# DLRM tower on one core: the feature products of four samples on quarters of the TensorE array instead of halves, in batches twice as large, and the first unit's gather ids loaded by themselves

## What is computed

```
e = jnp.stack([tbl_0[ids[:, 0]], ..., tbl_25[ids[:, 25]]], axis=1)
combined = jnp.concatenate([e, r_dense_x[:, None, :]], axis=1)
interact = jnp.einsum('bfd,bgd->bfg', combined, combined)
z = interact[:, _TRIU_I, _TRIU_J]
h = jnp.concatenate([z, r_dense_x], axis=1)
h = jnp.maximum(h @ W_top1 + b_top1, 0.0)
h = jnp.maximum(h @ W_top2 + b_top2, 0.0)
y = h @ W_top3
```

## Time and profile before

| | us |
|---|---|
| time, median of 3 runs | 375.73 (374.99 to 376.73) |
| time of the profiled execution | 375.79 |
| its span in the trace | 373.8 |
| PE busy | 333.4 (89%) |
| PEld busy | 315.3 (84%) |
| DVE busy | 247.8 (66%) |
| ACT busy | 203.4 (54%) |
| POOL busy | 252.8 (68%) |

### The profile page before, as it was taken

How to read it: one execution, slowest core, us unless ns; L and a number is a source line. 1 busy time by engine, 2 the same in 40 slices (tenths; PEclk the granted TensorE clock), 3 DMA queues, 4 the chain that set the end, 5 groups by cost and what they waited for, 6 DMA issues and landing times.

```text
span 373.8 us, 9779 instructions
## 1 busy us (share of the span) xinstructions
PE 333.4 (89%) x4178; PEld 315.3 (84%) x4178; DVE 247.8 (66%) x298; ACT 203.4 (54%) x274; POOL 252.8 (68%) x262
## 2 busy tenths in 40 slices
PE   0768759969999899989999999989998999989967
PEld 0768649869899898989899998989898989988955
DVE  3999805994469835895389735995389645980324
ACT  1575475425756448536755456645855466548322
POOL 3888777877777777777777777777777777760000
PEclk9998979989999999999999999999999999999989
DMA  7995324453154532563254623563255524420310
GB/s 238 392 322 166 97 59 132 107 156 84 51 131 121 162 81 69 155 184 85 53 155 100 175 63 91 143 180 80 56 155 147 136 51 119 113 72 2 87 39 0
DMA packets 32377, 44.92 MB, mean 120 GB/s; under 512 B 18791, under 2 KB 20463, under 8 KB 32334
## 3 DMA queue, kind: packets, MB, share of 16 engines
q1 hardware_dynamic: 23080, 25.82, 24.0%
q0 software_dynamic: 8192, 16.79, 17.6%
q10 hardware_dynamic: 1062, 1.69, 1.4%
HBM read 38.07 MB, written 6.20 MB: 118 GB/s over the span
## 4 chain that ended last, share of the span: by engine, by line
PE 49%; DVE 21%; POOL 10%; issue 8%; DMA 6%; SPq 3%; ACT 2%; ACTq 0%; DVEq 0%
DVE hot L689 18%; PE ps_gram L458 14%; POOL emb L402 10%; PE ps_mix L476 10%; PE ps_feat L440 7%; PE ps_feat L441 7%; PE ps_feat L426 4%; PE ps_mix L510 3%; DMA products_dram<-gram 3%; SPq L329 3%; ACT feat L588 1%; DMA idx<-in_ids 1%; PE ps_mix L515 1%; PE ps_feat L476 1%; PE ps_mix L525 1%
## 5 line engine op out<-in xcount | busy, mean ns | idle before, releaser
L402 POOL DMA_INDIRECT emb<-in_tbl,idx x256 | 252.1, 985 | 81.7 <-issue 76.8
L689 DVE TENSOR_TENSOR hot<-ids_row,ps_rows 128x1024 fp32r<-128x1024 int32 x160 | 186.2, 1215 | 19.1 <-PE ps_feat L441 16.1
L440 PE MATMUL ps_feat<-hot,held_h 128*128 128x256 f32 x640 | 164.8, 295 | 15.5 <-DVE held_l L675 11.7
L588 ACT COPY feat<-ps_feat 128x512 f32<-128x512 f32 x104 | 125.7, 1229 | 76.6 <-PE ps_feat L426 44.5
L441 PE MATMUL ps_feat<-hot,held_l 128*128 128x256 f32 x640 | 159.6, 287 | 0.0
L440 PEld LDWEIGHTS ps_feat<-hot,held_h 128*128 128x128 f32 x640 | 125.0, 195 | 17.8 <-issue 14.8
L441 PEld LDWEIGHTS ps_feat<-hot,held_l 128*128 128x128 f32 x640 | 125.2, 196 | 0.0
L458 PEld LDWEIGHTS ps_gram<-feat 128*54 128x54 f32 x2048 | 56.0, 132 | 9.7 <-issue 5.4
L458 PE MATMUL ps_gram<-feat 128*54 128x54 f32 x2048 | 61.0, 217 | 1.3 <-ACT feat L588 1.3
L426 PE MATMUL ps_feat<-ident,emb 128*128 128x128 f32 x256 | 40.8, 283 | 9.0 <-DMA emb<-in_tbl,idx 9.0
L603 ACT COPY gram<-ps_gram 119x432 f32<-119x432 f32 x64 | 35.2, 550 | 9.6 <-PE ps_gram L458 9.5
(11 more groups left out here) (101 smaller groups left out, 248.4 us busy)
## 6 DMA issues: line engine op xcount, KB each, us to landing
ids_row<-in_ids_h SPq DMA_DIRECT2D x40, 256.0 KB, 3.9
products_dram<-gram SPq DMA_DIRECT2D x30, 189.0 KB
held_raw<-in_held SPq DMA_DIRECT2D x8, 512.0 KB, 13.1
emb<-in_tbl,idx POOLq DMA_INDIRECT x256
z_raw<-products_dram SPq DMA_DIRECT2D x84, 26.0 KB
held_raw<-in_held ACTq DMA_DIRECT2D x2, 512.0 KB, 9.2
dense<-in_dense_t SPq DMA_DIRECT2D x8, 128.0 KB
w1z_raw<-in_W_top SPq DMA_DIRECT2D x3, 234.0 KB
```

The costliest lines, as they stand in the source:

```text
L402: pool.indirect_dma_start(emb[:, h, f, :], None, table, bass.IndirectOffsetOnAxis(ap=idx[:, i * UNIT + h, f:f + 1].bitcast(u32), axis=0),) ...
L440: nc.tensor.matmul(dst, held_h[:, o, c, :], hot[:, n % 2, c, :], start=c == 0, stop=False)
L588: nc.scalar.copy(feat_v[:, f, b], src).then_inc(act_out, 1)
L689: nc.vector.tensor_tensor(hot[:, n % 2, chunks, :], bass.AP(ids_row, (n % SLOTS) * UC, [[SLOTS * UC, HR], [0, PC], [1, UC]]), row_nums[:, ...
```

## The change

Three edits. The array is split in four column ranges instead of two (`SIDES = 4`): a matmul takes one sample, 27 columns, and its output starts at partition 0, 32, 64 or 96. A batch holds 16 groups of 4 samples instead of 8 (`GB = 16`), so that it fills 16 x 27 = 432 columns of a PSUM bank where it filled 8 x 54 = 432: 64 matmuls = 128 records a batch, and 4 batches and 4 copies a unit instead of 8. The gather ids of the first unit (2 of 16 columns of `idx`) are loaded by SP as its first transfer, ACT starts with table 0, and SP waits until table 0 has landed before it issues the other tables; the other ids follow behind table 2.

```diff
-    SIDES = 2
+    SIDES = 4
     PAIR = S // SIDES
     M = PAIR * F
     SIDE = 128 // SIDES
...
-    GB = 8
+    GB = 16
     BATCHES = UC // S // GB
...
+            sp.dma_start(idx[:, 0:UNIT, :], ids_g[:, 0:UNIT, :]).then_inc(first_ids_in, 16)
             load_ids_rows(0, 0)
+
+            sp.wait_ge(held_in[0], 16)
             for o in range(AHEAD, NH):
                 if o % PER_ROW == 0:
                     load_ids_rows(0, o // PER_ROW)
                 load_table(sp, o)
+                if o == AHEAD:
+                    sp.dma_start(idx[:, UNIT:, :], ids_g[:, UNIT:, :]).then_inc(other_ids_in, 16)
...
-            pool.wait_ge(ids_in, 16)
-            for i in range(UNITS):
+            pool.wait_ge(first_ids_in, 16)
+            gather(0)
+            pool.wait_ge(other_ids_in, 16)
+            for i in range(1, UNITS):
                 gather(i)
...
-            act.dma_start(idx[:], ids_g[:, :, :]).then_inc(ids_in, 16)
             for o in range(AHEAD):
                 load_table(act, o)
```

More of the change, by code:

```diff
@@ L209, in dlrm_tower_kernel @@
         row_nums = ps_rows[0:HR, 0, 0:HC].bitcast(i32)
-        ids_in = sem("ids_in")
+        first_ids_in = sem("first_ids_in")
+        other_ids_in = sem("other_ids_in")
         rows_in = [[sem(f"rows_in{h}_{w}") for w in range(NB)] for h in range(UNIT)]
```

## The result

| | before | after |
|---|---|---|
| time, median of 4 runs | 375.87 us | 396.03 us |
| ratio, 95% interval | | 1.0561 [1.0505, 1.0617] |
| span of the profiled execution | 373.8 us | 395.6 us |

5.6% slower, where 367.0 us was predicted. The profiled execution itself took 397.48 us.

What follows compares the result with a forecast made beforehand. PE with DVE was taken to pace the kernel at 41.33 us a unit, POOL close behind at 40.09. 375.79 - 5.39 - 1.65 - 2.0 + 0.3 = 367.05, predicted as 367.0 us, range 364.8 to 371.0.

Steps and rivals of the forecast that it cites:

- the term "Instructions": Last two batches, after `rows` 7: doubled product instructions might outrun their fetch, adding 0.3 us, bounds 0 and 1.
- Quarters: Product batches: a round of four matmuls takes 27.5 ns, bounds 25 to 40, so a batch takes 0.88 us.
- rival B: Product batches: four quarters no faster than two halves, PE stays the bound, 375.8 us, no change; chance 0.12.
- Ahead of `rows` 7 and from there on: PE's second phase, each unit: 0.86 us saved before `rows` 7 and 1.6 us from it to the next unit.
- The new wait for ACT's copy: Before the last two batches of a unit: PE waits about 0.8 us for ACT's feature copy.
- The copies: On ACT: 32 of 64 product copies of 0.55 us go; ACT keeps up, nothing added for it.
- POOL as the bound: Whole kernel: POOL's gathers become the bound and PE waits for `rows` 7; 367.0 us, chance 0.80.
- The sum 38.9 a unit: PE's time per unit after both savings, 41.33 - 0.86 - 1.6, under POOL's 40.09 us.
- the 5.39 and the 1.65 us: End of the kernel: PE's lateness at the last `rows` 7 removed, 5.39; `rows` 7 to the stores shortened by 1.65.
- First ids: Kernel start: a load an eighth as large lets POOL's first gather start 2.0 us earlier, bounds 0 and 2.4.
- Tables later: Unit 0: tables 2 to 9 and weights come some us later, at no cost or gain; collisions 1 us either way.
- Rival C: Product batches: a record costs 25 ns whatever its width, so slower, 424 us; chance 0.08.

Runs made afterwards that it cites:

- the added block above: 64 unread products of 27 columns (256 instructions) added to the ids-only kernel in each of units 1 to 6, ahead of the last four batches: 388.72 us, ratio 1.0387.

## Why the prediction was wrong

**The step that failed is the term "Instructions", + 0.3 us (bounds 0 and 1).** The prediction saw the packets and said that PE stops if the fetch doesn't keep up, but it priced this once, at the tail, by one more microsecond, and not at all in the units. Its own rows had the measure. 33 packets and 8356 PE instructions (2 x 4178, the profile's count) give 253 a packet; the four batches behind `rows` 7, 256 instructions, took 3.37 us, and nothing showed that instructions can come faster than that. Two batches, of 256 instructions and 0.88 us each, asked for almost four times that pace. The prediction read 3.37 us as a rate of the array alone.

What it cost: a unit has 512 more instructions, two blocks. From `rows` 4 of unit 2 to that of unit 6 a unit takes 44.7 us in the mean (43.7 to 45.4) instead of 41.33, 3.4 more. The columns saved on the array were real and went under: four undisturbed batches of 1.09 us instead of eight of 0.84, 2.4 us. So two blocks cost 5.8 us, 2.9 each with all that follows on them, near the 2.6 of the added block above. Over the whole kernel: at `rows` 4 of unit 2 the changed kernel is 5.3 us late (141.85 against 136.56) in spite of its earlier gathers, the four units from there on add 13.5, the stretch to `rows` 7 of unit 7 adds 3.5, and what follows takes 0.4 less. That is the 22 us.

**Quarters.** The guess of 27.5 ns for a round of four measured 34 ns (1.09 us for 32 rounds), inside the bounds of 25 to 40. Four quarters do work together; rival B is out. It counted for nothing, since the round was not what bound.

**Ahead of `rows` 7 and from there on.** In unit 1, 0.69 us more (94.85 to 101.88, against 6.34) where 0.86 less was forecast, and 1.8 more where 1.6 less was. The new wait for ACT's copy came as forecast, 0.73 us. The copies went as forecast too (32 less), and nothing came of it.

**POOL as the bound, and the tail.** The sum 38.9 a unit was never reached, so the 5.39 and the 1.65 us stayed out: from `rows` 7 to the stores the tail became 1.6 us longer. That the mechanism is right is shown by the kernel with half of the products: there the last gather's landing released `rows` 7, and its 365.17 us are near the forecast. It had fewer instructions, which the forecast overlooked.

**First ids.** The first gather starts 1.29 us earlier (4.13 against 5.42), not 2.0: the eighth of the load took 3.12 us, not the 2.03 of the small load at a quiet place. Its worth in time was measured alone as 2.1 us in the medians (0.2% to 0.8%, 0.7 to 2.9 us), and a head start of 1.3 lies in that. The old loads vary, too: in the profiled execution of the quarters without the new ones `idx` took 5.36 us and the first gather started at 6.38. **Tables later** cost nothing that shows.

**Rival C** had the sign and not the mechanism. It forecast 424 us from records that cost 25 ns whatever their width. A record costs 8.5 ns at the upper clock while there are instructions; what is fixed is the time of a block of 256. The 60 cycles a matmul of the Trainium skill, page TensorEngine Tiling (Array Packing), section "Instruction Overhead", are not what the trace shows, though its advice not to take a factor from a dimension that is already small would have been right here, for another reason.

**The clock** took a part that was not forecast. Between 85 and 361 us the kernel before had the upper level throughout; the changed one was granted the lower from 107.94 to 114.76, 155.72 to 159.14 and 288.84 to 292.26 us. The first of these follows on a stretch in which PE had stood still for 0.73 and then 1.59 us (the timeline above); the wait of 0.98 us lies in it. 13.7 us at half speed can cost 6.8 us at the most; how much they did cost of the 22 us was not separated.

**Still open:** why a packet starts only when the block before it has been at work for 1 us or more, and why PE then waits some 1.4 us more when it has landed, which together make 3.5 to 4 us of a transfer of about 1; and why starts of gathers pause PE in short matmuls for 0.25 us. No run here changes either.

## What to carry to other kernels

Count a change's instructions on an engine as a resource of its own. On PE, divide them by 256 and hold the time in which each block is worked off against 3.5 us: below that, narrower or more matmuls gain nothing, even where the array has room. Waits named "issue" inside a stream with no semaphore, with a packet of the instruction queue ahead of each end, are the sign; what helps is fewer or longer instructions there, since here only some two blocks had come ahead. An early small load of the ids that the pacing engine waits for is worth its head start.

## What the hardware did unexpectedly

- PE's instructions came in packets of 16 KB, 256 instructions, at 3.45 to 4.0 us a block in a stream of short matmuls (24 packets for 6144, 33 for 8356, 49 for 12452). The Trainium skill, page Runtime: NRT & Kernel Launch, section "Instruction fetch mechanics", has the same block of 16 KiB and 256 instructions, and calls the crossing of a boundary mostly hidden. The trace agrees on the size and disagrees on the hiding: fifteen waits of up to 2.5 us. The section gives PE room for 2048 instructions; here 223 records with their loads, under two blocks, ran before the first wait.
- fp32 matmuls of 27 columns on four quarters ran at 8.5 ns a record, 34 ns a round of four, at the upper clock, and 11.7 at the lower. Half the clock made them 1.4 times as long, not twice.
- ACT's write of the transposed features took 2.69 us in bf16 and 1.23 in fp32, in both with its elements 27 apart.
